# Chained top-k mask, attention, GRU and transformer block: how four stages hand over tiles

## The chip, the cores and the metric

The kernel runs on one core of a Trainium2 chip. The core has TensorE (matrix multiply), VectorE, ScalarE, GpSimd and SyncE, which issues the DMAs. The metric is the device time of one execution in microseconds (us), and lower is better. Times of a kernel are given as the median of its runs. One more execution is recorded by the hardware profiler, and all rows come from it.

## The reference, cut to what matters

Inputs: `x` is 4 x 512 x 512, float32 (B = 4 batches, T = 512 rows, D = 512 columns), with one side value per row and one condition vector per batch.

```python
x = x + top_k_mask(side * cond * softmax(x) / sqrt(512), k=5120)    # per batch: 1 where among the 5120 largest, diagonal left out
# small attention: 16 heads of 32
xn  = rms_norm(x, g_norm) * (1 + scale(cond)) + shift(cond)
q, k, v = split(xn @ W_qkv)                  # per head
q, k = rms_norm(q, g_q), rms_norm(k, g_k)
o = softmax(q @ k.T / sqrt(32)) @ v
x = x + o + o @ W_out
# GRU over the 512 rows, all batches in step, state h of 512
r = sigmoid(gi_r + (h @ W_hr + b_hr)); z = sigmoid(gi_z + (h @ W_hz + b_hz))
n = tanh(gi_n + r * (h @ W_hn + b_hn));  h = (1 - z) * n + z * h      # 512 steps, one after the other
x = x + all h
# transformer block: 16 heads of 128, MLP of 2048, all with condition-made shift, scale and gate
x1 = layernorm(x) * (1 + scale1) + shift1
x  = x + gate1 * (attention(x1 @ W_qkv + b) @ W_out + b_out)
x2 = layernorm(x) * (1 + scale2) + shift2
x  = x + gate2 * (gelu(x2 @ W_1 + b_1) @ W_2 + b_2)
```

## The kernel before

The program is a row of phases with a barrier between them: `topk_phase`, `small_attention_phase`, `split_weights`, `gate_input_phase`, `gru_phase`, `dit_condition_phase` and `dit_phase`. Each engine has its own instruction list in a phase and they meet by semaphores. A float32 operand of a product is held as a high and a low float16 part, and `products` (lines 400 to 402) does three matmuls for each product. A tile is 128 rows; a batch has TT = 4 tiles of rows and KD = 4 tiles of columns. `PE` is TensorE, `DVE` VectorE, `ACT` ScalarE, `POOL` GpSimd.

**Small attention** (from line 662). For each batch PE makes 12 projections into two PSUM banks in turn: q and k of tile 0, 1, 2, 3 (8 of them), then v of the four tiles. ACT copies each out (L903). For each tile POOL squares q and k together (L776) into the single buffer `small_tmp`, DVE sums the squares by head (L990) and adds the epsilon, ACT takes the root (L889), DVE inverts it and scales q and k (L1002, L1004, L1006). ACT then writes the high parts of q and of k, each twice (L897, four instructions), since a head's operand holds four slots of 32 columns. DVE writes the low parts, each twice (L1015, four instructions). The third v projection waits until DVE has read the first v out of its bank (L984). When all is there PE turns q and k of the first head (L818) and the heads run. POOL, after the squares of a batch, normalizes the rows of the next (L766) and then splits a quarter of the later weights (L1242, L1254, L1258) until the next batch's squares.

**GRU** (from line 1262). 512 steps. The columns of the state are two halves, a and b; the gates r, z, n of either half have a PSUM bank each. A step on PE is 4 matmuls that bring the input terms of r and z (L1334) and 96 matmuls of 4 or 8 columns with their own weight loads (L1343 low weights, L1353 high weights), in an order written out by hand: 48 before the last part of the state (`lo_b`) is needed, 48 after. DVE sums the parts of each bank (L1473, six times a step) into SBUF; for n the sum goes to `candidate`, beside the bias of h and the input term of n that ACT copied there (L1423). A scan over three slots for each value then makes `gi_n + r * sum` (L1477), ACT takes the tanh (L1431, L1438), and two more scans make the high float16 part of the new state (`hi_a`, `hi_b`, which PE waits for) and the float32 state.

**Transformer block** (from line 1616). One loop over four batches. `norm(...)` is done for all four tiles of a batch at once: statistics (L1910, L1914), root on ACT (L1853), `xn` (L1921), 16 transposes on PE (L1753), scale and shift (L1925), high part on ACT (L1856), low part on DVE (L1929). It runs twice in a batch: at its start on `X`, which SyncE loads when the previous batch's output is stored, and between the output projection of attention and the MLP. After the heads PE transposes the attended rows of tile t (L1817, 16 transposes) and projects tile t-1 (48 matmuls of 512 columns). DVE gates each projected tile (L1959), POOL adds the bias and X (L1735, L1737), and only when four tiles are there can the statistics end. Then the MLP: 16 groups of 12 matmuls of 512 columns, GELU on ACT (L1894), and a product of 48 matmuls for each tile, gated and added on DVE (L1983, L1987).

## Time and profile before

| | us |
|---|---|
| median of 3 runs | 4401.15 (4399.44 to 4403.91) |
| profiled execution | 4401.88 |
| its span, first to last instruction | 4400.2 |
| before the span's start and after its end | 1.7 |
| PE busy | 3783.8 (86%) |
| DVE busy | 2851.0 (65%) |
| ACT busy | 2073.5 (47%) |
| POOL busy | 518.8 (12%) |
| top-k | 0 to 311 |
| small attention | 311 to 1010 |
| weights and gate inputs | 1010 to 1188 |
| GRU | 1188 to 2639 |
| condition of the block | 2639 to 2704 |
| transformer block | 2704 to 4400 |

The stages are read from the first and last start of the instructions that belong to them. They follow one another, so each is a sum of its own: a stage is shorter only if the chain that ends it is. A row of a timeline is one instruction, or a run of like ones with their count; what stands in brackets is how long the engine had been idle and who ended that.

### The profile page before, as it was taken

What the parts mean: (1) busy time and instruction counts of PE and PEld (TensorE: products, weight loads), DVE (VectorE), ACT (ScalarE), POOL (GpSimd) and SP (SyncE); (2) the same over time, 40 slices, a digit from 0 to 9 for tenths busy, and PEclk for the clock granted to TensorE, in tenths of its full rate; (3) what the DMA queues carried; (4) which work ended last, traced back from release to release, by engine and by line L of the source; (5) the groups of instructions that cost most, each with busy time, mean ns of one, the idle gap of its engine ahead of it and who ended that gap; (6) DMA issues with size and microseconds to landing.
All of it is one profiled execution on the core that took longest, in us unless ns stands there. A gap on an engine that the chain in (4) does not pass through costs nothing. (4 is left out here: it accounts for less than half of the span.)

```text
span 4400.2 us, 179947 instructions
## 1 busy us (share of the span) xinstructions
PE 3783.8 (86%) x69948; PEld 2810.5 (64%) x69948; DVE 2851.0 (65%) x11559; ACT 2073.5 (47%) x7517; POOL 518.8 (12%) x425
## 2 busy tenths in 40 slices
PE   1527787776899999999999996998899889988998
PEld 0424464453599999999999992564366436634653
DVE  7888887885677777777777773573266227623752
ACT  2016585685755555555555550452154215422532
POOL 3007366360000000000000000001000100010001
PEclk9999998998855555555555558999899989998999
DMA  2002132131000000000000006200220121023102
GB/s 86 0 24 92 37 105 76 47 107 58 2 6 6 6 6 6 6 6 6 6 6 6 6 5 240 77 29 39 110 81 24 79 113 43 20 81 120 43 13 83
DMA packets 114609, 209.63 MB, mean 48 GB/s; under 512 B 44154, under 2 KB 76922, under 8 KB 112000
## 3 DMA queue, kind: packets, MB, share of 16 engines
q1 hardware_dynamic: 114436, 207.35, 13.7%
q8 instruction: 106, 1.74, 0.2%
q14 instruction: 67, 0.55, 0.0%
HBM read 165.35 MB, written 33.57 MB: 45 GB/s over the span
## 5 line engine op out<-in xcount | busy, mean ns | idle before, releaser
L514 ACT ACTIVATE dit_prob<-dit_bank,dit_head_nbias 128x512 f32<-128x512 f32 x256 | 176.0, 688 | 348.8 <-DVE dit_head_nbias L532 348.4
L1343 PE MATMUL gru_sum_na<-gru_state_parts,w_hh_lo 128*128 128x4 f16 x4096 | 262.3, 169 | 0.0
L1477 DVE TENSOR_TENSOR_SCAN gru_state_parts<-gru_keep_gate,gru_new_and_old 128x24 f16<-128x24 f32 x1024 | 212.7, 208 | 71.1
L1353 PE MATMUL gru_sum_na<-gru_state_parts,w_hh_hi 128*128 128x8 f16 x4096 | 254.9, 169 | 0.0
L1353 PE MATMUL gru_sum_ra<-gru_state_parts,w_hh_hi 128*128 128x8 f16 x4096 | 254.9, 169 | 0.0
L1353 PE MATMUL gru_sum_za<-gru_state_parts,w_hh_hi 128*128 128x8 f16 x4096 | 254.9, 169 | 0.0
L1343 PE MATMUL gru_sum_za<-gru_state_parts,w_hh_lo 128*128 128x4 f16 x4096 | 252.1, 166 | 0.0
L1343 PE MATMUL gru_sum_zb<-gru_state_parts,w_hh_lo 128*128 128x4 f16 x4096 | 252.1, 166 | 0.0
L1343 PE MATMUL gru_sum_nb<-gru_state_parts,w_hh_lo 128*128 128x4 f16 x4096 | 252.1, 166 | 0.0
L1343 PE MATMUL gru_sum_rb<-gru_state_parts,w_hh_lo 128*128 128x4 f16 x4096 | 252.1, 166 | 0.0
L1343 PE MATMUL gru_sum_ra<-gru_state_parts,w_hh_lo 128*128 128x4 f16 x4096 | 252.1, 166 | 0.0
L1477 DVE TENSOR_TENSOR_SCAN gru_n_in<-gru_reset_gate,gru_candidate 128x24 f32<-128x24 f32 x1024 | 213.0, 208 | 45.9
L1353 PE MATMUL gru_sum_nb<-gru_state_parts,w_hh_hi 128*128 128x8 f16 x4096 | 236.8, 169 | 0.0
L1473 DVE TENSOR_REDUCE gru_r_in<-gru_sum_ra 128x8 f32<-128x16 f32 x512 | 89.7, 175 | 224.0 <-PE gru_sum_ra L1353 224.0
L1731 POOL TENSOR_TENSOR dit_gated_bias<-dit_gates,dit_bias_rows 128x1024 f32<-128x1024 f32 x4 | 9.4, 2342 | 1906.9 <-DMA dit_gates<-gates 1906.9
L1441 ACT ACTIVATE gru_hist<-gru_state 128x16 f32 x512 | 118.8, 232 | 232.9 <-DVE gru_state L1477 232.9
L496 PE MATMUL small_bank<-ident,small_prob 128*128 128x128 f32 x1024 | 167.7, 288 | 68.9 <-DVE small_turned L631 43.8
L208 PE MATMUL edge_part<-ones,edge_mask 128*128 128x1 f16 x2176 | 79.7, 166 | 160.1 <-DVE edge_mask L297 152.4
L1666 PE MATMUL dit_bank<-dit_qk 128*128 128x512 f16 x768 | 207.6, 379 | 1.4 <-DVE dit_qk L1941 1.4
L400 PE MATMUL dit_bank<-dit_yh,dit_w_qk 128*128 128x512 f16 x512 | 194.1, 379 | 6.9 <-DVE dit_V L1936 6.9
L1343 PEld LDWEIGHTS gru_sum_na<-gru_state_parts,w_hh_lo 128*128 128x128 f16 x4096 | 188.1, 105 | 17.6
L625 ACT ACTIVATE small_prob<-small_bank,small_head_nmax 128x512 f32<-128x512 f32 x256 | 176.5, 690 | 42.9 <-DVE small_head_nmax L526 38.0
(315 smaller groups left out, 13410.5 us busy)
## 6 DMA issues: line engine op xcount, KB each, us to landing
dit_w_qk<-w_qk_parts SPq DMA_DIRECT2D x64, 512.0 KB, 3.6
weights<-w_parts SPq DMA_DIRECT2D x8, 4096.0 KB, 12.1
weights<-w_out_parts SPq DMA_DIRECT2D x5, 4096.0 KB, 17.5
...
```

Source lines behind the costliest of these rows:

```text
L208: mm = pe.matmul(part[g][:, j:j + 1], mask[:, g * 2 + j, c * P:(c + 1) * P], const["ones16"][:, 0:1], start=(c == 0), stop=(c == E // P - 1))
L400: pe.matmul(out, lh, rh, start=start, stop=False)
L496: mm = pe.transpose(self.PT[t % 2][:, s * P:(s + 1) * P], self.prob[:, t % 2, s * P:(s + 1) * P], self.ident)
L514: act.activation(self.prob[:, t % 2, :], self.S[t % 2], ACT.Exp, bias=bias[:, t:t + 1], scale=self.scale, accum_out=self.rsum[:, t:t + 1]) ...
L625: act.activation(self.prob[:, t % 2, :], self.S[t % 2], ACT.Exp, bias=self.nmax[:, t:t + 1], accum_out=self.rsum[:, half, j:j + 1]).then_i ...
L1343: mm = pe.matmul(bank[:, j * 2 * B:j * 2 * B + B], w_hh[1][:, k, c:c + P], parts[:, par, 0, k, :, LAST], start=opens, stop=False, skip_gro ...
L1353: mm = pe.matmul(bank[:, j * 2 * B:(j + 1) * 2 * B].rearrange("p (e b) -> p e b", e=2), w_hh[0][:, k, c:c + P], parts[:, par, :, k, :, LAS ...
L1441: act.activation(hist[:, :, :, at(i)].rearrange("p f b o -> p f (b o)"), state[:, 1 - par, :, :, LAST], ACT.Copy).then_inc(kept, 1)
L1473: return dve.tensor_reduce(out, columns.rearrange("p (f e b) -> p f b e", e=2, b=B), AX.X, ALU.add)
L1477: return dve.tensor_tensor_scan(line(out), line(factor), line(term), 0.0, ALU.mult, ALU.add)
L1666: mm = pe.matmul(s, qk[:, hs.parity, 0, qe, t * P:(t + 1) * P], qk[:, hs.parity, 1, ke, :], start=(qe + ke == 0), stop=(qe == 1))
L1731: pool.tensor_tensor(gb[:], gates[:], rows[:], ALU.mult).then_inc(gated, 1)
```

## The change

There are four parts; arithmetic and results are meant to be the same.

1. **Top-k phase.** Two small parameter loads and the making of the condition's scale and shift move here from the start of small attention. DVE prepares factors (5 small instructions after the search), ACT applies them as it reads the sums out of PSUM (8 small instructions).
2. **Small attention.** The squares move from POOL to ACT, one instruction each for q and k. The second copy of each low part is an ACT copy of the first and no longer a second DVE subtraction. POOL begins a batch's share of rows and weights only when the batch's low parts are done, so beside the heads.
3. **GRU.** The n banks hold four values for each output: the two sums that PE writes, the bias, and the input term, which ACT writes into PSUM for the next step. The scan runs over these four directly (with factors 0, 1, 1, r). DVE's two sums into `candidate` and their waits go. The order of the 96 matmuls is new: 44 stand before `lo_b` is needed, 52 after, and the second half of n is wholly at the end.
4. **Transformer block.** The second norm goes tile by tile between the output projections: the transposes of tile t-1 stand in the middle of the projection of tile t, and the first four MLP groups are done for the first 384 columns before the last tile's 128. The row tile's bias and X are added beforehand. The first norm of the next batch is done before and during the MLP product of the present one, from a second buffer `given` that SyncE fills early. The last batch is written out apart from the loop.

```diff
 topk_phase
+            for f in range(2 * KD):
+                act.activation(mod[:, f, :], emb_sum[:, f, :], ACT.Identity, scale=emb_scale[:, f:f + 1],
+                               bias=emb_shift[:, f:f + 1]).then_inc(mod_made, 1)
...
 small_attention_phase, POOL
             for b in range(B):
-                for t in range(TT):
...
-                    pool.tensor_tensor(tmp[:].rearrange("p a d -> p (a d)"), raw[:, t].rearrange("p a d -> p (a d)"),
-                                       raw[:, t].rearrange("p a d -> p (a d)"), ALU.mult).then_inc(square_ready, 1)
+                pool.wait_ge(lo4_done, (b + 1) * TT * 2)
                 if b + 1 < B:
                     norm_rows(b + 1)
                 store.pool(pool, b)
 small_attention_phase, ACT
+                def low_again(t):
+                    for j, dst in enumerate((q4, k4)):
+                        act.wait_ge(lo4_done, b * TT * 2 + t * 2 + j + 1)
+                        src, to = (2, 3) if j == 0 else (1, 3)
+                        act.activation(dst[:, t, :, to, :], dst[:, t, :, src, :], ACT.Copy).then_inc(lo4_again, 1)
...
                     act.activation(dst, qkv_bank[n % 2][:], ACT.Copy, scale=scale).then_inc(bank_free, 1)
+                    if j < QK:
+                        act.wait_ge(bank_free, b * 12 + n + 3)
+                        if j == 0:
+                            act.wait_ge(ssq_ready, b * TT + t + 1)
+                        act.activation(tmp[:, j, :], dst, ACT.Square).then_inc(square_ready, 1)
                     if QK <= n < first_v:
                         (root, high_parts)[j](t - 1)
+                    if n > QK and n < first_v and j == 0:
+                        low_again(t - 2)
                     if n == first_v:
                         root(TT - 1)
+                        low_again(TT - 2)
                     if n == first_v + 1:
                         high_parts(TT - 1)
+                low_again(TT - 1)
 gru_phase, PE (a step)
+                    low(rb, R_GATE, second, first, par)
+                    low(za, Z_GATE, first, first, par)
+                    low(ra, R_GATE, first, first, par)
+                    low(zb, Z_GATE, second, first, par)
+                    pe.wait_ge(gn_ready, i + 1)
+                    low(na, N_GATE, first, first, par, opens=True)
                     pe.wait_ge(lo_a, i + 1)
+                    high(za, Z_GATE, first, first, par)
+                    high(na, N_GATE, first, first, par)
+                    high(ra, R_GATE, first, first, par)
                     pe.wait_ge(hi_b, i + 1)
+                    low(ra, R_GATE, first, second, par)
+                    high(zb, Z_GATE, second, first, par)
+                    low(za, Z_GATE, first, second, par)
                     pe.wait_ge(lo_b, i + 1)
+                    high(ra, R_GATE, first, second, par).then_inc(ra_sum, 1)
+                    high(na, N_GATE, first, second, par)
+                    high(za, Z_GATE, first, second, par).then_inc(za_sum, 1)
+                    low(rb, R_GATE, second, second, par)
+                    low(na, N_GATE, first, second, par).then_inc(na_sum, 1)
+                    high(zb, Z_GATE, second, second, par)
+                    high(rb, R_GATE, second, first, par)
+                    high(rb, R_GATE, second, second, par).then_inc(rb_sum, 1)
+                    low(zb, Z_GATE, second, second, par).then_inc(zb_sum, 1)
+                    high(nb, N_GATE, second, second, par, opens=True)
+                    low(nb, N_GATE, second, second, par)
+                    high(nb, N_GATE, second, first, par)
+                    low(nb, N_GATE, second, first, par).then_inc(nb_sum, 1)
 gru_phase, ACT (between the keep gate and the tanh of half a)
+                    copy_gi_n(i + 1, 1 - par)
 gru_phase, DVE
+                    dve.wait_ge(r_a, i + 1)
                     dve.wait_ge(na_sum, i + 1)
-                    total(cand[:, par, A, :, 0], na_bank).then_inc(u_a, 1)
-                    dve.wait_ge(r_a, i + 2)
-                    dve.wait_ge(u_a, i + 2)
-                    dve.wait_ge(gn_ready, i + 2)
-                    chain(n_in[:, A], reset[:, A], cand[:, par, A]).then_inc(n_in_a, 1)
+                    chain(n_in[:, A], reset[:, A], n_terms[:, par, 0]).then_inc(n_in_a, 1)
...
                     chain(new_parts[:, 0, A], keep[:, A], mix[:, A]).then_inc(hi_a, 1)
+                    chain(new[:, A], keep[:, A], mix[:, A]).then_inc(state_a, 1)
                     dve.wait_ge(nb_sum, i + 1)
-                    total(cand[:, par, Z, :, 0], nb_bank).then_inc(u_b, 1)
 dit_phase, PE
+                for t in range(1, TT):
+                    if t + 1 < TT:
+                        turn_heads(t + 1)
+                    project_out(t, low_heads)
+                    turn_tile(t - 1)
+                    project_out(t, high_heads)
...
+                pe.wait_ge(tile_yl, b * TT + TT - 1)
+                for j in range(4):
...
+                    hidden(j, j, 0, early)
+                    if j == 1:
+                        turn_tile(TT - 1)
+                pe.wait_ge(tile_yl, b * TT + TT)
+                for j in range(4):
+                    hidden(j, j, early, T).then_inc(hid_sum, 1)
...
+                for t in range(TT):
+                    pe.wait_ge(mlp_gated, b * TT + t + 1)
...
+                    mm.then_inc(mlp_sum, 1)
+                    if t == 0 and more:
+                        turn_rows(b + 1)
 dit_phase, DVE
+                low_heads(0)
+                low_heads(1)
+                add_attention(0)
+                for t in range(1, TT):
+                    if t + 1 < TT:
+                        low_heads(t + 1)
+                    modulated_tile(t - 1)
+                    add_attention(t)
+                modulated_tile(TT - 1)
...
+                if more:
+                    normed_rows(b + 1)
                 for t in range(TT):
                     dve.wait_ge(mlp_sum, b * TT + t + 1)
...
+                    if t == 0 and more:
+                        modulated_rows(b + 1)
```

`add_attention(t)` gates a tile, adds X, takes its statistics, asks ACT for the root and writes `xn` of the tile; `modulated_tile(t)` applies scale and shift to four 128 x 128 squares and, after ACT's high part, writes the low part. The first projection of a batch's v now waits for the last gated tile of the batch before (`mlp_gated`).

## Rows read from the trace of the kernel before

**Rows 1.** Windows: stretch, its length, busy us of PE, PEld, DVE, ACT, POOL, clock, DMA.

```profile
330.00:383.50 53.50, 35.36 (x144) 14.40 (x144) 39.01 (x45) 17.53 (x34) 29.93 (x21) 0.87 0.10 30
...
3016.70:3034.60 17.90, 3.54 (x17) 3.17 (x16) 14.58 (x23) 4.01 (x6) 12.97 (x10) 0.69 0.58 234
...
1188.00:2639.00 1451.00, 1445.61 (x51200) 1420.94 (x51200) 1080.47 (x8210) 848.79 (x5121) 0.00 (x0) 0.50 0.03 6
```

**Rows 2.** Timeline of all engines, one GRU step.

```profile
1801.97 0.27 PE L1343 MATMUL gru_sum_na<-gru_state_parts,w_hh_lo 128*128 128x4 f16 x4
...
1803.27 0.25 PE L1353 MATMUL gru_sum_ra<-gru_state_parts,w_hh_hi 128*128 128x8 f16 x4
...
1803.56 0.17 DVE L1473 TENSOR_REDUCE gru_r_in<-gru_sum_ra 128x8 f32<-128x16 f32 x1 [0.44 <-PE gru_sum_ra L1353]
...
1803.76 0.21 ACT L1426 ACTIVATE gru_reset_gate<-gru_r_in 128x8 f32<-128x8 f32 x1 [0.17 <-DVE gru_r_in L1473]
...
1804.04 0.21 DVE L1477 TENSOR_TENSOR_SCAN gru_n_in<-gru_reset_gate,gru_candidate 128x24 f32<-128x24 f32 x1
...
1804.28 0.22 ACT L1431 ACTIVATE gru_new_and_old<-gru_n_in 128x8 f32<-128x8 f32 x1
...
1804.53 0.21 DVE L1477 TENSOR_TENSOR_SCAN gru_state_parts<-gru_keep_gate,gru_new_and_old 128x24 f16<-128x24 f32 x1
...
1804.79 0.27 PE L1343 MATMUL gru_sum_na<-gru_state_parts,w_hh_lo 128*128 128x4 f16 x4
```

**Rows 3.** Waits of PE in the block: us in total, times, longest us.

```profile
PE dit_bank L1753 <- DVE dit_big L1921: 107.5, 8, 17.6
```

**Rows 4.** Timeline, PE, from attention's output to the MLP of the first batch.

```profile
2967.39 4.52 PE L1817 MATMUL dit_bank<-ident,dit_big 128*128 128x128 f32 x32 [0.45 <-DVE dit_big L546]
...
3016.46 0.38 PE L402 MATMUL dit_bank<-weights,dit_qk 128*128 128x512 f16 x1
...
3034.61 0.61 PE L400 MATMUL dit_bank<-dit_yh,weights 128*128 128x512 f16 x1 [3.84 <-DVE dit_yl L1929]
...
3040.80 0.38 PE L400 MATMUL dit_bank<-dit_yh,weights 128*128 128x512 f16 x1
```

**Rows 5.** Timeline, PE and DVE, from the first batch of the block to the second.

```profile
3124.67 0.38 PE L402 MATMUL dit_bank<-weights,dit_V 128*128 128x512 f16 x1
...
3125.09 0.69 DVE L1983 SCALAR_TENSOR_TENSOR dit_prob<-dit_bank,dit_gates 128x512 f32<-128x512 f32 x1 [8.84 <-PE dit_bank L402]
...
3148.41 0.61 PE L400 MATMUL dit_bank<-weights,dit_yh 128*128 128x512 f16 x1 [3.71 <-DVE dit_yl L1929]
...
3153.37 0.38 PE L400 MATMUL dit_bank<-weights,dit_yh 128*128 128x512 f16 x1
```

**Rows 6.** Timeline of small attention's first batch: ACT, POOL, DVE and PE.

```profile
334.73 0.60 ACT L903 ACTIVATE small_raw<-small_bank 128x512 f32<-128x512 f32 x1 [4.51 <-PE small_bank L402]
...
343.18 2.08 POOL L776 TENSOR_TENSOR small_tmp<-small_raw 128x1024 f32<-128x1024 f32 x1 [3.24 <-ACT small_raw L903]
...
343.43 2.38 DVE L1006 TENSOR_TENSOR small_raw<-small_raw,small_rq 128x512 f32<-128x512 f32 x1
...
383.61 0.38 PE L818 MATMUL small_qbank<-ident,small_q 128*128 128x128 f16 x4 [1.69 <-DVE small_vl L984]
```

**Rows 7.** Groups by line in small attention: count, busy us, mean ns, idle before.

```profile
L903 ACT ACTIVATE small_raw<-small_bank 128x512 f32<-128x512 f32 x32 | 18.8, 588 | 57.1 <-PE small_bank L402 57.1
L897 ACT ACTIVATE small_q<-small_raw 128x512 f16<-128x512 f32 x32 | 18.4, 621 | 31.1 <-DVE small_raw L1004 31.1
L990 DVE TENSOR_REDUCE small_ssq<-small_tmp 128x32 f32<-128x1024 f32 x16 | 19.4, 1212 | 35.2 <-POOL small_tmp L776 35.2
L1002 DVE TENSOR_TENSOR small_raw<-small_raw,small_rq 128x512 f32<-128x512 f32 x16 | 11.1, 692 | 0.6
L867 ACT ACTIVATE small_tmp<-X 128x512 f32 x16 | 10.1, 630 | 41.6 <-PEq L59 39.5
```

**Rows 8.** Groups by line, DVE, 300 to 312: count, busy us, mean ns.

```profile
L377 DVE TENSOR_TENSOR_SCAN edge_rank<-edge_key,edge_before,edge_zeros 128x512 f32<-128x512 f32 x3 | 3.8, 1277 | 0.0
```

475 lines of the change are left out of this document (262 added, 213 removed).

## The prediction

> **What bounds the kernel now.** I read the windows by stage first, then the waits of PE, then the timelines around the places where PE stands still. The stages follow one another, so each is judged by its own chain.
>
> In the GRU PE is busy 1445.61 of 1451.00 us, at a granted clock of 0.50, the lower level of 1.2 GHz [rows 1]. Busy PE is not proof of a bound, so the timeline of one step decides: the step starts with the low matmuls of na at 1801.97 and the next one at 1804.79, 2.82 us later [rows 2]. In it 48 matmuls run from 1801.97 to 1803.27, 27 ns each. After 1803.27 there are 48 more and 4 that bring inputs, 52 x 27 ns = 1.40 us, but the next step starts only after 1.52. So PE waits about 0.12 us a step for the chain of the gates: PE and that chain are nearly level.
>
> In the transformer block PE stands still at two kinds of places. Its transposes of the normed rows waited 107.5 us for DVE in 8 waits [rows 3]: twice a batch, once between the output projection of attention and the MLP, and once at the start of a batch. The first is 17.9 us long with PE busy for 3.54 and DVE for 14.58 [rows 1, 4], the second runs from 3124.67 to 3148.41 [rows 5]. After either stall the matmuls run slower: 512 columns take 0.41 us each in the mean of the first 15 ((3040.80 - 3034.61)/15) and again 0.41 in the first 12 of the next batch ((3153.37 - 3148.41)/12), and 0.216 from there on.
>
> In small attention the projections of a batch are bound by neither of these: PE is busy 35.36 of 53.50 us, DVE 39.01 [rows 1]. From the first copy out of PSUM at 334.73 to the turning of the first head at 383.61 there are 48.9 us [rows 6], while PE needs 12 x 12 x 0.216 = 31.1 for the matmuls. The chain is the one of the squares, sums, scales and parts of each tile, on DVE, ACT and POOL. The heads after it are not touched.
>
> **Top-k and the condition.** DVE gets five small instructions on its path, some 0.2 us each; small attention loses about as many from its start, but there ACT's squares of rows set the start anyway. Sum: +1 us, from 0 to +2.
>
> **Small attention.** The POOL squares leave. Their price is double: the instruction itself (2.08 us), and DVE's product beside it, 2.38 us at 343.43 for a form that has a mean of 0.69 in the same stage [rows 6, 7]. The Trainium skill, SBUF — State Buffer (SBUF: two separate sides), says that GpSimd and a VectorE instruction with two SBUF inputs exclude each other for a whole instruction; with the rows either way, it only says why, and that the block's head instructions, which read PSUM, would not suffer from the POOL work that now lies fully beside them.
>
> The new turn of a tile, from DVE's sum of one tile to that of the next, is a chain across ACT and DVE, since there is one buffer of squares: sum 1.21, square of the next q 0.63, two second low copies 2 x 0.59, copy of the next k 0.59, its square 0.63, four high copies 4 x 0.62, the last low part 0.69. That is 7.4 us [rows 7]; ACT's second low copies are new, priced as the copy of the same size. The first sum starts one projection, a copy and a square after 334.73's counterpart: 2.6 + 0.59 + 0.63 = 3.8. Three turns are 22.2, with 0.6 for the first, which waits for PE. The last tile: sum 1.21, root and inversion about 0.7 (estimate), three products 2.07, low part of v 0.69, then the two v projections that had to wait, 5.2, a copy and a low part 1.28, and 0.3 to the turning: 11.4. Sum 38.0 against 48.9, so 10.9 less a batch, 4 x 10.9 = 43 us. Bounds: if nothing but the two excluded instructions is saved the gain is 20; if PE were the bound, 31.1 + 3, it is 59. I take 43. POOL now begins the weights when the low parts are done. Its quarter must end before the next batch's heads; it had over 50 us of room, and only the rows of the next batch (four instructions) are needed before, at the end of the heads. What is behind its new wait is hidden.
>
> **GRU.** The chain that ends late, read as starts in the timeline [rows 2]: ra matmuls 1803.27, sum 1803.56, sigmoid 1803.76, scan 1804.04, tanh 1804.28, scan of the high part 1804.53, PE 1804.79. In steps: 0.29 + 0.20 + 0.28 + 0.24 + 0.25 + 0.26 = 1.52.
> - The scan no longer waits for a second sum of DVE itself. It goes by the sigmoid, which lets a follower go 0.25 after its start, as the tanh does: -0.03. The last na matmuls start 16 x 27 = 0.43 after ra's; 0.29 later is 0.72, when the sigmoid is ready (0.29 + 0.20 + 0.25 = 0.74). So no new wait.
> - The scan has 32 elements for 24. A scan of 512 takes 1277 ns and one of 24 takes 0.21 us [rows 2, 8], 2.2 ns an element, so +0.02. It reads PSUM, which no scan in this trace does: from 0 to +0.10; I take +0.02, since the sum of 16 from PSUM takes only 0.17.
> - ACT copies the next input term just before the tanh: the tanh waits perhaps 0.04. The trace has no write of ACT into PSUM. The Trainium skill, ScalarE: Activation LUTs (Step-by-step: what each stage is for), calls PSUM the faster destination; no row here shows it.
>
> So the chain is 1.52 - 0.03 + 0.04 + 0.04 = 1.57 and PE's own 52 + 4 matmuls are 56 x 27 = 1.51: the wait of PE is nearly gone because eight matmuls more fit behind the ra sum. Before `lo_b` 44 matmuls are left: 1.19. Step: 1.57 + 1.19 = 2.76, or 2.74 if the copy is hidden. Late next would be `lo_b`: its chain begins with the scan of nb at 1.57 (nb's last group at 1.29, + 0.28), then tanh 0.26, high scan 0.25, state scan and subtraction 0.34, and 0.22 to PE: 2.64, needed at 2.74. It fits by 0.1. I take 2.75, and for the step before the mean of 2.82, as shown, and 1451.00/512 = 2.83: 0.078 x 512 = 40 us less. Bounds: PE's floor is 100 x 27 = 2.71, 56 us less; with the two unknown costs at their ends, 0.
>
> **Transformer block.** (a) Between projection and MLP: PE's last matmul starts at 3016.46, so PE is free at 3016.68; the MLP starts at 3034.61 [rows 4]: 17.9 us. The 16 transposes remain, now between projections: 4.52/32 x 16 = 2.3. The first 15 MLP matmuls take 6.19 us where 15 x 0.216 = 3.24 would do, and these 2.95 go with the stall. 17.9 - 2.3 + 2.95 = 18.6. What covers the moved work: DVE has a projection of 48 x 0.216 = 10.4 plus 4.5 us of transposes for a tile, and its work for one (four low parts 2.8, gating, addition, statistics, `xn` about 3.9, the tile's scale and low part 2) is about 9. `xn` of a tile is ready 3.9 us after its projection, needed at 5.2 in mid-projection. For the last tile two partial MLP groups, 2 x 12 x 0.162 = 3.9, lie before its transposes, so the wait is 0 to 0.5, and two more groups cover the rest. 384 and 128 columns cost the same as 512. Sum: 4 x 18.6 = 74.
> (b) From batch to batch: PE is free at 3124.89 and restarts at 3148.41, 23.5 us [rows 5]. What stays is the wait for the last gating (3125.09 + 0.69, so 0.9 to 1.0) and 2.3 of transposes; with 3153.37 - 3148.41 = 4.96 for 12 matmuls that cost 2.5 at 0.216, another 2.4 goes. 23.5 - 1.0 - 2.3 + 2.4 = 22.6, three times: 68. The load of X, some 6 us of the stall, is done during the heads. DVE's norm stands before the gating of the MLP's first tile, 10.4 us of PE time, and takes about 6; scale and parts take another 6, during the second tile.
> Sum 142. Bounds: if the clock drops all the same, 7 x 2.7 = 19 less; if each handover waits 1 to 2 us, 12 less; so 111. Upward 147. Last batch and first start keep their time.
>
> **The sum.** Profiled execution 4401.88 (span 4400.2 and 1.7 around it; the median is 4401.15): + 1 - 43 - 40 - 142 = 4177.9; from the median, 4177.
>
> **Rivals.**
> - Forecast: all parts come about as costed, 4177 (4145 to 4210). Chance 0.62.
> - The GRU gives nothing: PSUM scan and ACT's copy take the 0.06 to 0.10 that the order brings. For it: both costs are unseen in this trace and the chain has no room. Against: the sums of DVE read PSUM in 0.17. 4177 + 40 = 4217, with a small rest lost elsewhere up to 4250. Chance 0.22.
> - The handovers move more than they give: tile norms wait and the clock falls again, 31 us in the block; the ACT chain in small attention gives only 20, 23 more: 4231. For it: ACT has 10 instructions in a turn. Chance 0.09.
> - The clock in the GRU rises. The Trainium skill, TensorE: Matmul & The Clock Gate (Part 1: The HAM clock gate), ties the full clock to sustained activity, and by that rule PE should long be at 2.4 GHz here; the rows show 0.50 with PE busy for 99.6%, so the trace disagrees. As a mechanism of this kernel: with the 0.12 us wait gone the clock goes to 1.00, PE's side halves and the chains remain, 1.26 to the high scan of a and at least 1.2 from it to `lo_b`: a step of 2.46. Then 0.28 x 512 = 145 more: about 4030. Chance 0.02.
> - PE's floor everywhere: GRU 56, small attention 59: 4177 - 16 - 16 = 4145 or less. Chance 0.02 beyond the forecast's range.
> - Slower than before: the n scan waits for PSUM. If reading the n bank costs a step over 0.08 us the GRU loses, and the whole loses only when that cost reaches (4401 - 4177)/512 = 0.44 us. A scan of 0.65 us for 0.21 would do it; at a cost of 0.50 the time is 4177 + 256 = 4433. Nothing in the trace has such a price. Chance 0.03, a third of it within 0.2%.
> - It doesn't do what it says: the first-tile MLP wait or the weight load of `w_v` keeps the batches apart. That load starts when the last MLP group is done, 45 us ahead; 4177 + 68 = 4245. It is in the third case's chance.
>
> The forecast's own range, the second and third case and PE's floor together need 4130 to 4250; below it stands a GRU at 2.4 GHz, above it the sums of two failures and the slower case. A measurement of this kernel tells 0.2%, 9 us, from no change. Faster 0.97, same 0.01, slower 0.02.
>
> **What would show it.** GRU steps of about 2.74 us with PE starting its low matmuls within 0.05 of the last bring; the n scan at 0.23 to 0.25 us; six DVE sums become four. PE's waits on norm transposes from 107.5 us to under 20, and 0.216 spacing right at the start of the MLP and of the later batches. Projections of a small-attention batch in 42 to 44 us and L1006's counterpart at 0.69. Wrong would be: a clock other than 0.50 in the GRU, an n scan over 0.3 us, or PE waiting for ACT's second low copies long after the last v.

## The result, and the profile after

The changed kernel takes 4211.17 us (median of 4, 4207.77 to 4212.9); the kernel before, beside it, 4402.53 (4399.44 to 4406.57). The ratio is 0.9565, 95% interval 0.9552 to 0.9578. The forecast was 4177 in a range of 4130 to 4250: the direction and the size hold, and 34 us of the gain are missing. The time alone does not single out the forecast: it lies 1 us above the forecast's own 4145 to 4210 and 6 us below the rival in which the GRU gives nothing (4217). The stages do. The profiled execution took 4210.57, its span 4208.9.

The stages come one after the other, so the difference of the spans, 191.3 us, splits without a rest. Each stage is cut at rows that both traces have: ACT's first squares of X (before 311.23, after 312.22), ACT's first and last tanh of the GRU, which writes `new_and_old` (1194.42 and 2638.09; 1159.41 and 2575.18), PE's first projection of the block (2723.87; 2665.57), and the end of the span.

| stretch | before | after | difference | forecast |
|---|---|---|---|---|
| top-k, to the first squares | 311.2 | 312.2 | +1.0 | +1 |
| small attention, weights, gate inputs | 883.2 | 847.2 | -36.0 | -43 |
| GRU loop, first to last step | 1443.7 | 1415.8 | -27.9 | -40 |
| last step to the block's first projection | 85.8 | 90.4 | +4.6 | 0 |
| block, to the end | 1676.3 | 1543.3 | -133.0 | -142 |

No single term failed by much; four each gave less than their price. The windows of the changed kernel (stretch, length, busy us of PE, PEld, DVE, ACT, POOL, clock, DMA) answer [rows 1]:

```profile
330.44:375.64 45.20, 35.31 (x152) 14.85 (x153) 23.48 (x40) 26.64 (x51) 8.40 (x8) 0.95 0.01 3
1159.00:2575.00 1416.00, 1414.52 (x51134) 1403.67 (x51131) 1039.92 (x7162) 824.67 (x5118) 0.00 (x0) 0.50 0.03 6
2960.75:2969.30 8.55, 8.55 (x55) 5.18 (x54) 5.18 (x12) 2.12 (x3) 0.78 (x1) 1.00 0.93 368
3050.90:3052.00 1.10, 0.01 (x1) 0.02 (x2) 0.97 (x2) 0.00 (x0) 0.00 (x0) 1.00 0.08 15
```

The first is batch 0 of small attention, from the first projection to the first score product: VectorE is busy for half of it. The second is the GRU, still at a clock of 0.50, the level of 1.2 GHz. The third is the passage from attention's output to the MLP, where TensorE stood still for most of 17.9 us and is now busy throughout. The fourth is a batch boundary: 1.1 us of idleness where 23.5 were lost [rows 5].

One step of the GRU, timeline of all engines, answers [rows 2]:

```profile
1903.21 0.25 PE L1366 MATMUL gru_sum_ra<-gru_state_parts,w_hh_hi 128*128 128x8 f16 x4
...
1903.49 0.17 DVE L1495 TENSOR_REDUCE gru_r_in<-gru_sum_ra 128x8 f32<-128x16 f32 x1 [0.44 <-PE gru_sum_ra L1366]
...
1903.70 0.22 ACT L1446 ACTIVATE gru_reset_gate<-gru_r_in 128x8 f32<-128x8 f32 x1 [0.51 <-DVE gru_r_in L1495]
...
1903.99 0.22 DVE L1499 TENSOR_TENSOR_SCAN gru_n_in<-gru_reset_gate,gru_sum_n 128x32 f32<-128x32 f32 x1
...
1904.13 0.17 ACT L1435 ACTIVATE gru_sum_n<-gi_n 128x16 f32 x1
...
1904.24 0.22 ACT L1452 ACTIVATE gru_new_and_old<-gru_n_in 128x8 f32<-128x8 f32 x1
...
1904.49 0.21 DVE L1499 TENSOR_TENSOR_SCAN gru_state_parts<-gru_keep_gate,gru_new_and_old 128x24 f16<-128x24 f32 x1
...
1904.76 0.27 PE L1356 MATMUL gru_sum_rb<-gru_state_parts,w_hh_lo 128*128 128x4 f16 x4
...
1905.95 0.25 PE L1366 MATMUL gru_sum_ra<-gru_state_parts,w_hh_hi 128*128 128x8 f16 x4
```

From ra to the low matmuls are 1.55 us (forecast 1.57), from there to the next ra 1.19 (forecast 1.19): 2.74. The step inside the loop is what was forecast. But the mean of the loop is 1415.8/511 = 2.77. TensorE's first bring (the matmul that brings the input terms) of each step shows where the rest is:

```profile
1899.16 0.19 PE L1339 MATMUL gru_sum_za<-gru_gi_now,gru_scaled_ident 128*128 128x16 f16 x1
...
1901.85 0.17 PE L1339 MATMUL gru_sum_za<-gru_gi_now,gru_scaled_ident 128*128 128x16 f16 x1
...
1904.60 0.17 PE L1339 MATMUL gru_sum_za<-gru_gi_now,gru_scaled_ident 128*128 128x16 f16 x1
...
1907.33 0.17 PE L1339 MATMUL gru_sum_za<-gru_gi_now,gru_scaled_ident 128*128 128x16 f16 x1
...
1910.23 0.19 PE L1339 MATMUL gru_sum_za<-gru_gi_now,gru_scaled_ident 128*128 128x16 f16 x1
```

Steps of 2.69, 2.75, 2.73 and 2.90 us: the fourth goes over the end of TensorE's loop, which holds four steps. The bring after it starts early again, so the price of the edge is read from the chain, at ACT's tanh of half a:

```profile
1909.73 0.22 ACT L1452 ACTIVATE gru_new_and_old<-gru_n_in 128x8 f32<-128x8 f32 x1
...
1912.57 0.22 ACT L1452 ACTIVATE gru_new_and_old<-gru_n_in 128x8 f32<-128x8 f32 x1
```

These two lie 2.84 us apart, across an edge. Over the whole loop the starts of this tanh are 2.746 us apart inside TensorE's loop and 2.838 across its end: an edge costs 0.09 us. In the kernel before every step has 2.823, edge or not.

In the block, PE's waits (total, times, longest) answer [rows 3]:

```profile
PE dit_bank L1789 <- DVE dit_big L2022: 21.8, 1, 21.8
...
PE dit_bank L414 <- DMA dit_w_qk<-w_qk_parts: 4.3, 3, 2.2
```

The eight waits of 107.5 us are down to the one at the block's start (21.8, where the prediction's sign was under 20), and a new one has come: for the weights of head 2. The timeline of SyncE's queue shows what is ahead of them, and TensorE's rows the wait, in batches 0 and 2:

```profile
2708.66 0.33 SPq L1731 DMA_DIRECT2D weights<-w_parts  x1
2709.31 0.40 SPq L1735 DMA_DIRECT2D dit_given_x<-x_gru  x1
2715.91 0.35 SPq L1721 DMA_DIRECT2D dit_w_qk<-w_qk_parts  x1
```

```profile
2725.85 0.39 PE L414 MATMUL dit_bank<-dit_yh,dit_w_qk 128*128 128x512 f16 x1 [0.98 <-DMA dit_w_qk<-w_qk_parts]
...
3497.14 0.39 PE L414 MATMUL dit_bank<-dit_yh,dit_w_qk 128*128 128x512 f16 x1 [2.25 <-DMA dit_w_qk<-w_qk_parts]
```

The 1 MB of the next batch's rows (`given`) is new between the MLP's weights and head 2's. The last batch has no such load and no such wait.

At the block's start the first norm is slower. DVE and POOL after:

```profile
2652.59 1.26 POOL L1768 TENSOR_TENSOR dit_gated_bias_rest<-dit_gated_bias 128x512 f32<-128x512 f32 x1
2653.81 5.65 POOL L1772 TENSOR_TENSOR dit_X<-dit_given_x,dit_gated_bias 128x512 f32<-128x512 f32 x4
```

```profile
2653.03 5.31 DVE L2022 TENSOR_SCALAR dit_big<-dit_given_x,dit_mv,dit_rstd 128x512 f32<-128x512 f32 x4
```

Before, the same four `xn` took 1.91 us there, where GpSimd was idle, and 5.12 in the middle of the batch, where it worked:

```profile
2714.64 1.91 DVE L1921 TENSOR_SCALAR dit_big<-dit_X,dit_mv,dit_rstd 128x512 f32<-128x512 f32 x4
...
3022.19 5.12 DVE L1921 TENSOR_SCALAR dit_big<-dit_big,dit_mv,dit_rstd 128x512 f32<-128x512 f32 x4
```

So the price stood in the trace of before; the forecast did not look for what the moved GpSimd work would lie beside.

### The profile page after: what moved, and what is told of

Its sections match the earlier page's. It is cut to its first block and busy times, and to the rows that moved or that the text cites. A ratio compares the mean times of both kernels' runs of the same rounds, so it can differ in the third digit from the quotient of the medians.

```text
span 4208.9 us, 177781 instructions
## 1 busy us (share of the span) xinstructions
PE 3731.0 (89%) x70140; PEld 2793.1 (66%) x70140; DVE 2778.2 (66%) x10585; ACT 2086.6 (50%) x7601; POOL 461.4 (11%) x397
## 5 line engine op out<-in xcount | busy, mean ns | idle before, releaser
L1366 PE MATMUL gru_sum_n<-gru_state_parts,w_hh_hi 128*128 128x8 f16 x8192 | 500.2, 175 | 0.0
L1356 PE MATMUL gru_sum_n<-gru_state_parts,w_hh_lo 128*128 128x4 f16 x8192 | 489.4, 168 | 0.0
L1366 PEld LDWEIGHTS gru_sum_n<-gru_state_parts,w_hh_hi 128*128 128x128 f16 x8192 | 376.7, 104 | 0.0
L1356 PEld LDWEIGHTS gru_sum_n<-gru_state_parts,w_hh_lo 128*128 128x128 f16 x8192 | 376.7, 104 | 0.0
L1499 DVE TENSOR_TENSOR_SCAN gru_n_in<-gru_reset_gate,gru_sum_n 128x32 f32<-128x32 f32 x1024 | 225.5, 220 | 54.6
L1356 PE MATMUL gru_sum_rb<-gru_state_parts,w_hh_lo 128*128 128x4 f16 x4096 | 261.3, 169 | 0.0
L1366 PE MATMUL gru_sum_zb<-gru_state_parts,w_hh_hi 128*128 128x8 f16 x4096 | 254.5, 169 | 0.0
L1446 ACT ACTIVATE gru_reset_gate<-gru_r_in 128x8 f32<-128x8 f32 x512 | 111.4, 218 | 272.5 <-DVE gru_r_in L1495 272.5
L414 PE MATMUL dit_bank<-weights,dit_V 128*128 128x512 f16 x512 | 196.5, 384 | 10.3 <-DVE dit_V L2115 10.3
```

The costliest lines, as they stand in the source:

```text
L414: pe.matmul(out, lh, rh, start=start, stop=False)
L1356: mm = pe.matmul(columns[:, j, 0], w_hh[1][:, k, c:c + P], parts[:, par, 0, k, :, LAST], start=opens, stop=False, skip_group_check=True)
L1366: mm = pe.matmul(columns[:, j], w_hh[0][:, k, c:c + P], parts[:, par, :, k, :, LAST], start=opens, stop=False, skip_group_check=True)
L1446: act.activation(reset[:, A, :, GATED], r_in[:, A], ACT.Sigmoid, scale=1.0 / GS).then_inc(r_a, 1)
L1499: return dve.tensor_tensor_scan(line(out), line(factor), line(term), 0.0, ALU.mult, ALU.add)
```

## Experiments

Every kernel was read in its own stage, cut as in the table above. The GRU repeats best: the eight kernels with the changed GRU loop have it at 1415.8 to 1416.3 us. Where nothing was changed in them, the start of the block takes 89.5 to 90.4 us, the block 1540.9 to 1543.3, small attention with weights and gate inputs 845.7 to 850.7, and its four batches together 177.0 to 179.3 us to their first scores, of which the changed kernel has the lowest. So a difference of 2 us in that sum is no effect.

**1. The loop edge: `edge8`.** TensorE's loop of the GRU holds 8 steps.

```diff
 gru_phase
-        NOW = 2
+        NOW = 4
```

> The changed kernel, with TensorE's loop in the GRU holding 8 steps instead of 4 (64 loop edges for 128). Theory (loop edge): in the trace of the changed kernel three of four steps take 2.69 to 2.75 us and the one across the loop edge 2.91, so an edge costs about 0.13 us that the old chain used to hide; 64 edges fewer give 64 x 0.13 = 8 us: GRU loop 1415 to about 1407 us, whole 4211 to about 4203. Rival (chain): the 0.024 us a step over 2.745 is spread over all steps as a longer gate chain, and the time stays at 4211. Rival (code): the longer loop body brings its instructions slower and the GRU gets slower than 1415.

Measured: 4201.46 us (4200.14 to 4202.63), ratio to before 0.954 (0.9524 to 0.9555). The GRU loop is 1407.5, 8.3 less, as the first theory said. The price by edge was not as it said: the step across an edge now takes 2.796 us and the others 2.746, so an edge of the longer loop costs 0.05 us where the shorter one's cost 0.09. 127 edges of 0.092 are 11.7 us and 63 of 0.050 are 3.2: 8.5 less, for the 8.3 measured. 0.13 is only what went for each edge that is gone. Why the edge of the longer loop is cheaper stays open. The edit also halves the number of loads of input terms that TensorE waits for, but in the changed kernel the step with such a wait and no edge takes 2.745 us, so that wait costs nothing. Another 2.4 us are in the block, where nothing was changed (see experiment 2 for what varies there).

**2. The new load: `given_late`.** The rows of the next batch are loaded after the heads' weights.

```diff
 dit_phase, SyncE
-                if more:
-                    sp.wait_ge(a_begun, (b + 1) * TT)
-                    sp.wait_ge(xn_ready, (b + 1) * TT)
-                    sp.dma_start(given[:], ...)
                 with sp.Fori(0, (H - 2) // 2) as pair:
...
+                if more:
+                    sp.wait_ge(a_begun, (b + 1) * TT)
+                    sp.wait_ge(xn_ready, (b + 1) * TT)
+                    sp.dma_start(given[:], ...)
```

> The changed kernel with the load of the next batch's rows (1 MB) issued after the heads' weight loads instead of between the 4 MB load of the MLP weights and the load of head 2's weights. Theory (queue): the rows stand ahead of head 2's weights and delay them; TensorE waits 1.0, 1.1 and 2.25 us for them in three batches, and the heads take 1.2, 1.3 and 4.1 us longer than before: all of 6.6 us goes, whole about 4204, no wait of TensorE on those weights. Rival (the 4 MB load alone does it): the wait stays at about 1 us each and the time at 4209 to 4211.

Measured: 4201.59 us (4200.64 to 4202.4), ratio 0.9539 (0.9523 to 0.9555). TensorE waits for no head's weights. From the first head's projection to the second MLP product the batches take 294.3, 294.3, 294.3 and 294.2 us, in the changed kernel 295.4, 295.5, 298.4 and 294.2: 6.5 us, the number of the theory. Of these 4.3 are the waits themselves; after the longest one, 2.25 us in batch 2, the matmuls came 0.43 us apart from 3498.04 on, for 0.216, which is most of the rest. The block gains 11.3 in all (1543.3 to 1532.0). The other 4.8 lie behind another wait: the MLP's second product begins after 2.6 us of idleness in both kernels, and in the changed one seven or eight matmuls near its start come 0.43 us apart in batches 0, 1 and 3, in this one they all come at 0.216. Windows of PE (length, busy, clock, DMA) over those matmuls, first the changed kernel, then this one:

```profile
3005.80:3012.00 6.20, 6.20 (x21) 0.72 0.98 423
...
3778.75:3789.10 10.35, 10.35 (x48) 1.00 0.83 356
```

```profile
3007.74:3014.00 6.26, 6.26 (x29) 1.00 0.97 419
```

The same idleness lets the clock fall in one batch and not in the next. What decides it isn't settled; it makes the block vary by a few us between kernels that don't touch it.

**3. GpSimd beside the first norm: `pool_waits`.**

```diff
 dit_phase, GpSimd
                 pool.wait_ge(gated, b * 2 + 1)
+                pool.wait_ge(yl_ready, (b + 1) * KD)
                 pool.tensor_tensor(gb_rest[:], gb[:, 1, :], gb[:, 0, :], ALU.subtract).then_inc(gated, 1)
```

> The changed kernel, in the block: GpSimd's additions of bias and rows (one of the two biases, then four tiles) wait until VectorE has the low parts of the normed rows. Theory (shared port): in the changed kernel the four xn of the first batch take 5.31 us beside these additions and took 1.91 before; they go back to 1.9, TensorE's first projection of the block comes 3.4 us earlier after the last GRU step (90.4 to about 87 us), whole about 4207. Rival (memory): the xn are slow because the new loads write into SBUF at that time; nothing changes, 90 us.

Measured: 4208.32 us (one run). The stretch before the block's first projection is 86.7 for 90.4 (89.5 to 90.4 in the kernels that leave it alone), and the four `xn` are back:

```profile
2654.26 1.91 DVE L2023 TENSOR_SCALAR dit_big<-dit_given_x,dit_mv,dit_rstd 128x512 f32<-128x512 f32 x4
```

The loads are the same in both, so it is GpSimd's work. The Trainium skill, SBUF — State Buffer (Who interferes with whom), says that `tensor_scalar` can run in a mode that takes the port pair shared with GpSimd, so that the later of the two waits for the whole instruction. The trace agrees: 5.31 and 5.12 us beside GpSimd, 1.91 and 1.91 without. The forecast had drawn on this page only for instructions with two inputs.

**4. The order of the GRU's matmuls undone, the scan kept: `scan_old_order`.** The 96 matmuls, and DVE's two sums of rb and zb, stand as before: 48 matmuls ahead of `lo_b`, na right after ra and za, nb in two places.

```diff
 gru_phase, PE
-                    low(rb, R_GATE, second, first, par)
-                    low(za, Z_GATE, first, first, par)
-                    low(ra, R_GATE, first, first, par)
-                    low(zb, Z_GATE, second, first, par)
                     pe.wait_ge(gn_ready, i + 1)
                     low(na, N_GATE, first, first, par, opens=True)
+                    low(rb, R_GATE, second, first, par)
+                    low(zb, Z_GATE, second, first, par)
+                    low(nb, N_GATE, second, first, par, opens=True)
+                    low(ra, R_GATE, first, first, par)
+                    low(za, Z_GATE, first, first, par)
...
```

> The changed kernel with the order of the GRU's 96 matmuls (and of the two sums of rb and zb) as in the kernel before; the scan over PSUM stays. Theory (order pays): the gate chain stays at 1.55 us and 48 matmuls instead of 44 stand before lo_b, 1.30 for 1.19 us: step 2.85, GRU loop about 1456 us (after: 1415, before: 1443), whole about 4252: the scan in PSUM without the order is worth nothing or less. Rival (scan pays): what helped is that VectorE makes two sums fewer; the order matters little, GRU loop 1415 to 1420, whole 4211 to 4216.

Measured: 4235.99 us (one run), GRU loop 1439.1, a step of 2.81. It is neither theory's number, but the order carries most: 23.3 of the 27.9 us go with it, and the scan alone is worth 4.6. Inside TensorE's loop the order is worth more, 2.813 for 2.746 or 34 us; 11 of them are paid at the loop edges, which the old order hides (2.818 across an edge). The expected 1456 took the chain of the new order, 1.55; in this order it is shorter:

```profile
1802.64 0.25 PE L1366 MATMUL gru_sum_ra<-gru_state_parts,w_hh_hi 128*128 128x8 f16 x4
...
1803.38 0.22 DVE L1499 TENSOR_TENSOR_SCAN gru_n_in<-gru_reset_gate,gru_sum_n 128x32 f32<-128x32 f32 x1 [0.18 <-ACT gru_reset_gate L1446]
...
1804.15 0.27 PE L1356 MATMUL gru_sum_n<-gru_state_parts,w_hh_lo 128*128 128x4 f16 x4
```

The scan comes 0.74 after ra, right behind the sigmoid, and the low matmuls after 1.51. In the new order it came after 0.78: there the last matmuls of na begin at 1903.63, later than here (1802.85, 0.21 after ra). So the new order pays about 0.04 for na's place and wins 4 matmuls, 0.11, ahead of `lo_b`.

**5. The new order without the scan: `order_alone`.** The kernel before with the new order; DVE still sums n into SBUF.

```diff
 gru_phase, PE and DVE of the kernel before
+                    low(rb_bank, R_GATE, second, first, par)
+                    low(za_bank, Z_GATE, first, first, par)
...
+                    high(ra_bank, R_GATE, first, second, par).then_inc(ra_sum, 1)
+                    high(na_bank, N_GATE, first, second, par)
...
+                    low(nb_bank, N_GATE, second, first, par).then_inc(nb_sum, 1)
...
+                    chain(new[:, A], keep[:, A], mix[:, A]).then_inc(state_a, 1)
                     dve.wait_ge(nb_sum, i + 1)
                     total(cand[:, par, Z, :, 0], nb_bank).then_inc(u_b, 1)
```

> The kernel before with the new order of the 96 matmuls in the GRU and VectorE's work in the matching order; n is still summed into SBUF by VectorE. Theory (the scan makes the order possible): nb now ends the step, and its sum (about 0.2 us) lies before the scan of n, so the low part of b is ready 2.64 + 0.2 = 2.84 us after the ra matmuls begin: step 2.83 to 2.86, GRU loop 1443 to 1460 us, no gain over the kernel before (whole 4400 to 4420). Rival (order alone pays): step 2.75 or less, GRU loop about 1410 to 1415, whole about 4373.

Measured: 4514.31 us (one run), GRU loop 1554.9, 111 more than before. The theory's direction holds, its size doesn't. The step is 3.04, not 2.84:

```profile
1803.90 0.25 PE L1353 MATMUL gru_sum_ra<-gru_state_parts,w_hh_hi 128*128 128x8 f16 x4
...
1804.61 0.18 DVE L1473 TENSOR_REDUCE gru_candidate<-gru_sum_na 128x8 f32<-128x16 f32 x1
...
1804.87 0.21 DVE L1477 TENSOR_TENSOR_SCAN gru_n_in<-gru_reset_gate,gru_candidate 128x24 f32<-128x24 f32 x1
...
1805.63 0.27 PE L1343 MATMUL gru_sum_rb<-gru_state_parts,w_hh_lo 128*128 128x4 f16 x4
```

The sum of na, which the old order hid behind the sigmoid, now starts at the sigmoid's end: the scan comes 0.97 after ra and the low matmuls 1.73. The second half is late as well, 1.31 for 1.19; nb's sum, now at the end of the order, lies ahead of it. So the two edits of the GRU don't add: +111 and -4.6 alone, -27.9 together. The scan is what makes the order possible.

**6. The squares back on GpSimd: `pool_squares`.** ScalarE's squares and GpSimd's wait go, GpSimd's loop over tiles is as before. So GpSimd's rows and weights, too, lie beside VectorE's work again.

```diff
 small_attention_phase
             for b in range(B):
-                pool.wait_ge(lo4_done, (b + 1) * TT * 2)
+                for t in range(TT):
+                    pool.wait_ge(bank_free, b * 12 + place_of[t, 1] + 1 + 2)
+                    pool.wait_ge(ssq_ready, b * TT + t + 1)
+                    pool.tensor_tensor(tmp[:].rearrange("p a d -> p (a d)"), raw[:, t].rearrange("p a d -> p (a d)"),
+                                       raw[:, t].rearrange("p a d -> p (a d)"), ALU.mult).then_inc(square_ready, 1)
...
-                        act.activation(tmp[:, j, :], dst, ACT.Square).then_inc(square_ready, 1)
...
```

> The changed kernel with the squares of small attention back on GpSimd (one instruction a tile into the same buffer, and GpSimd's rows and weights right after them, as before); ScalarE keeps the second low copies. From the first projection of a batch to its first score product the changed kernel takes 45.2, 43.8, 44.0 and 44.1 us, the kernel before 54.9, 53.6, 53.6 and 51.2. Theory (squares): nearly all of the difference is the square and the product that stands still beside it, so 8 to 9 us a batch come back, 52 to 54 us, whole 4240 to 4246. Rival (VectorE's load): the squares are half of it, 4 to 5 us a batch, whole about 4229.

Measured: 4227.4 us (one run). The batches take 51.4, 48.5, 49.5 and 48.2 us to their first score: 6.2, 4.7, 5.5 and 4.1 more, 20.5 together. This is the rival's number. By groups of DVE (count, busy us, mean ns, idle before), the product beside the square, first in the changed kernel, then here:

```profile
L1014 DVE TENSOR_TENSOR small_raw<-small_raw,small_rq 128x512 f32<-128x512 f32 x16 | 10.9, 683 | 0.0
```

```profile
L1014 DVE TENSOR_TENSOR small_raw<-small_raw,small_rq 128x512 f32<-128x512 f32 x16 | 33.0, 2060 | 0.0
```

The mechanism is as told, 0.68 us becomes 2.06, but it is not the whole: squares and exclusion, with GpSimd's rows and weights beside VectorE (its low parts take 0.87 and 0.93 us for 0.69), are a little over half of the small part's gain.

**7. The second low copies back on VectorE: `copies_on_dve`.**

```diff
 small_attention_phase, DVE
-                        slot = 2 if j == 0 else 1
-                        dve.tensor_tensor(dst[:, t, :, slot, :], src, dst[:, t, :, 0, :], ALU.subtract)\
-                           .then_inc(lo4_done, 1)
+                        for e in range(2):
+                            slot = 2 + e if j == 0 else 1 + 2 * e
+                            ins = dve.tensor_tensor(dst[:, t, :, slot, :], src, dst[:, t, :, 0, :], ALU.subtract)
+                        ins.then_inc(lo4_done, 1)
...
 small_attention_phase, ACT
-                    if n > QK and n < first_v and j == 0:
-                        low_again(t - 2)
...
```

> The changed kernel with the second low copies of q and k in small attention back on VectorE as second subtractions; squares stay on ScalarE. Theory (a chain that alternates): a tile's turn gives 2 x 0.61 us of ScalarE for 2 x 0.69 of VectorE, nearly level; projections to first score 44 to 46 us a batch, whole 4211 to 4216. Rival (VectorE is the bound): its 2 x 0.69 us a tile come on top, 5.5 us a batch, 49 to 50 us, whole about 4232.

Measured: 4217.91 us (one run); batches of 47.9, 46.4, 45.8 and 44.6 us, 7.6 together. It lies between, near the first theory. The first score again comes 1.37 us after the turning, for 1.80. With experiment 6 that makes 28 of the 36.3 us of the four batches. The rest, 8 us, was not taken apart; experiment 6 has GpSimd's rows and weights back in their place already, so it belongs to the two edits together (in the kernel before VectorE's doubled low parts lie beside GpSimd and take 0.91 and 0.99 us each), if it is not scatter.

**8. The weights beside the products: `weights_early`.** GpSimd's wait for the low parts goes.

```diff
 small_attention_phase, GpSimd
             for b in range(B):
-                pool.wait_ge(lo4_done, (b + 1) * TT * 2)
                 if b + 1 < B:
                     norm_rows(b + 1)
                 store.pool(pool, b)
```

> The changed kernel without GpSimd's wait for the low parts: a batch's share of rows and weights starts with the projections and lies beside VectorE's products instead of beside the heads. Theory (exclusion): each of VectorE's 20 instructions with two SBUF inputs of a batch waits about 1 us for a GpSimd instruction (0.6 to 1.5 us each); its products take 1.2 to 2 us for 0.69, a batch's projections 55 to 65 us for 44, whole 4255 to 4290. Rival (no contention of that size): the products stay at 0.7 us and the time at 4208 to 4213.

Measured: 4233.18 us (one run), small attention and gate inputs 870.9 for 847.2. A batch takes 50.4, 48.7, 47.6 and 45.2 us to its first score, and the first three periods from batch to batch are 7.9 to 8.4 longer. It is neither theory's number: contention is there, and the whole loses 22 us where at least 44 were expected, so the waits aren't one whole instruction each. Means over four batches, in the last of which GpSimd has little to do, by groups of DVE:

```profile
L1013 DVE TENSOR_TENSOR small_raw<-small_raw,small_rq 128x512 f32<-128x512 f32 x16 | 15.6, 976 | 0.0
...
L1000 DVE TENSOR_SCALAR small_ssq<-small_ssq 128x32 f32<-128x32 f32 x16 | 11.4, 710 | 0.6
```

The smallest instruction suffers most: the scalar step on 32 elements takes 710 ns, and 181 in the changed kernel, where GpSimd waits.

**9. The next batch's norm after the MLP: `serial_rows`.** The calls for norm, transposes and parts of batch b + 1 stand behind the last tile of the MLP on TensorE and VectorE; ScalarE's come in the same order as before.

```diff
 dit_phase, PE
-                    if t == 0 and more:
-                        turn_rows(b + 1)
+                if more:
+                    turn_rows(b + 1)
 dit_phase, DVE
-                if more:
-                    normed_rows(b + 1)
                 for t in range(TT):
...
-                    if t == 0 and more:
-                        modulated_rows(b + 1)
+                if more:
+                    normed_rows(b + 1)
+                    modulated_rows(b + 1)
```

> The changed kernel with the first norm of the next batch (VectorE's norm, the 16 transposes, scale and parts) after the MLP's last tile instead of beside the MLP product; its rows are still loaded early. Theory (the norm was the stall): a boundary gets back the gating and sum 1.4, the norm 5.9, transposes to first projection 7.4 us, less 3.0 that stand there now, and 0 to 2.4 for the lower clock: 12 to 15 us each, three times 36 to 45; where GpSimd's additions fall beside the xn, 3.4 more each. Whole 4247 to 4266. Rival (the load was the stall): since the rows lie in SBUF early, under 5 us a boundary, whole under 4226.

Measured: 4262.45 us (one run), block 1594.5, 51.2 more. A boundary costs 17.1: 14.9 to the first projection and 2.2 of slower matmuls in it (the first one; 51.2 is three times this). The norm was the stall, not the load. GpSimd's additions fell beside the low parts instead of `xn`, 5.76 us for 2.49, the same price at another place; without these 3.3 us a boundary is within the theory's 12 to 15.

**10. Undivided MLP groups: `whole_groups`.**

```diff
 dit_phase, PE
-                pe.wait_ge(tile_yl, b * TT + TT - 1)
+                turn_tile(TT - 1)
+                pe.wait_ge(tile_yl, b * TT + TT)
                 for j in range(4):
...
-                    hidden(j, j, 0, early)
-                    if j == 1:
-                        turn_tile(TT - 1)
-                pe.wait_ge(tile_yl, b * TT + TT)
-                for j in range(4):
-                    hidden(j, j, early, T).then_inc(hid_sum, 1)
+                    hidden(j, j, 0, T).then_inc(hid_sum, 1)
```

> The changed kernel with the first four MLP groups undivided: TensorE transposes the last tile right after its projection and begins the groups with all 512 columns when that tile's low part is ready. Theory (cover): from the last projection's end at 2960.97 to the end of the last low part at 2968.35 are 7.4 us, which 48 matmuls of 384 columns cover now; without them the stall is 6.7 us a batch and up to 2.9 more if the clock falls: 27 to 38 us, whole 4238 to 4249. Rival (tile norms alone suffice): under 2 us a batch, whole under 4219.

Measured: 4242.06 us (one run), block 1576.6, 33.3 more. The two waits of the first batch are those of the sum:

```profile
2965.07 0.63 PE L1864 MATMUL dit_bank<-ident,dit_big 128*128 128x128 f32 x4 [3.86 <-DVE dit_big L2083]
...
2968.62 0.61 PE L414 MATMUL dit_bank<-dit_yh,weights 128*128 128x512 f16 x1 [2.92 <-DVE dit_yl L2094]
```

From the transposes of the first head rows to the second MLP product, the cut by which the middle gained 73 us (see below), the batches take 104.6, 104.4, 104.4 and 105.4 us for 95.4: 37 us hang on the division of the first four groups, at the upper end of the theory's 27 to 38. The block grew by less because other places ran faster: the slow matmuls of experiment 2 came in batch 3 alone, and the heads lost 4.8 us to their weights for 6.5. The other 36 us are left to the norm by tiles by subtraction; no run has it alone.

**11. Three edits at once: `all_three`.** Those of experiments 1, 2 and 3 together.

```diff
-        NOW = 2
+        NOW = 4
...
+                pool.wait_ge(yl_ready, (b + 1) * KD)
...
                 with sp.Fori(0, (H - 2) // 2) as pair:
...
+                if more:
...
+                    sp.dma_start(given[:], ...)
```

> The changed kernel with three edits at once: TensorE's GRU loop of 8 steps, the next batch's rows loaded after the heads' weights, and GpSimd's additions after the low parts. They lie in different stages, so they add: 8.3 (measured in the GRU alone) + 6.5 (three waits on head 2's weights) + 3.5 (xn beside GpSimd) = 18 us, and 0 to 5 from matmuls at the lower clock after short stalls: 4188 to 4193. Rival (they overlap): more than 4196.

Measured: 4190.22 us (4188.57 to 4195.27), ratio 0.9519 (0.9503 to 0.9535). GRU loop 1406.1, start of the block 86.7, block 1534.8: they add. It is faster than both kernels of the comparison, 21 us under the changed one.

**12. A still longer loop: `all_three_16`.**

```diff
-        NOW = 4
+        NOW = 8
```

> As the kernel with three edits, with TensorE's GRU loop of 16 steps. Theory (loop edge): 32 edges fewer than with 8 steps, 0.13 us each, 4 us less: GRU loop 1403, whole 4184 to 4189. Rival (code): bringing the longer loop body costs as much as the edges, so the GRU loop stays at 1407 or grows.

Measured: 4459.12 us (4446.26 to 4460.47), ratio 1.0119 (1.0102 to 1.0136): slower than the kernel before. The GRU loop is 1678.2. The step across an edge takes 8.41 us in the mean, which makes some 176 of the 272 us that the GRU lost; the rest is lost inside the loop. TensorE's 188 waits of over 0.3 us have no other engine behind them ("issue"), and there is none of that length in the GRU with a loop of 4 or 8 steps. The queue that brings instructions (packets, MB, share) has five times the bytes, first the kernel with 8 steps, then with 16:

```profile
q8 instruction: 114, 1.87, 0.2%
```

```profile
q8 instruction: 557, 9.13, 0.8%
```

```profile
1841.38 0.19 PE L1339 MATMUL gru_sum_za<-gru_gi_now,gru_scaled_ident 128*128 128x16 f16 x1 [3.10 <-issue]
...
1844.82 0.19 PE L1366 MATMUL gru_sum_zb<-gru_state_parts,w_hh_hi 128*128 128x8 f16 x1 [2.13 <-issue]
```

The rival was right, far beyond its own words. A step has 100 matmuls and 100 weight loads in the trace (51200 of each in 512 steps, [rows 1]), so 8 steps are 1600 of these and 16 are 3200. The Trainium skill, Runtime: NRT & Kernel Launch (Instruction fetch mechanics), gives TensorE room for 2048 instructions and says that a taken branch whose target isn't in the part held waits for a DMA. The trace agrees with that: 114 packets with the loop of 8, and 557 with 16, 14 more for each of the 32 turns. Where between 1600 and 3200 the limit lies, no run here shows.

## Why the prediction was right, and where it fell short

**Top-k, +1.** Right: +1.0.

**Small attention, -43; measured -36.0.** The step that was mis-sized is "4 x 10.9": the price of batch 0 was taken four times. From first projection to first score the batches took 54.9, 53.6, 53.6 and 51.2 before, and 45.2, 43.8, 44.0 and 44.1 after: 9.7, 9.8, 9.7 and 7.2 less. Within batch 0 the sum was close: 38.0 forecast from the first copy to the turning of head 1, and 373.84 - 334.89 = 38.95 measured. Timelines of ACT, DVE and PE in that batch:

```profile
334.89 0.60 ACT L912 ACTIVATE small_raw<-small_bank 128x512 f32<-128x512 f32 x1 [4.35 <-PE small_bank L416]
...
369.38 0.60 ACT L912 ACTIVATE small_vh<-small_bank 128x512 f16<-128x512 f32 x1 [3.21 <-PE small_bank L416]
```

```profile
338.77 1.22 DVE L998 TENSOR_REDUCE small_ssq<-small_tmp 128x32 f32<-128x1024 f32 x1 [7.71 <-ACT small_tmp L917]
...
360.43 1.21 DVE L998 TENSOR_REDUCE small_ssq<-small_tmp 128x32 f32<-128x1024 f32 x1
```

```profile
373.84 0.38 PE L821 MATMUL small_qbank<-ident,small_q 128*128 128x128 f16 x4 [1.91 <-ACT small_k L907]
```

The first sum came after 3.9 us (forecast 3.8), three turns took 21.7 (22.2 and 0.6), the last tile 13.4 instead of 11.4. The two last projections of v were taken at 2.6 us each, but the first of them runs after 5.4 us of idleness: its copy starts 4.07 us after it, at 369.38 (it began at 365.31), and the next one 2.59 later. Before had the same stretch at the same length (8.58 us from this projection to the turning, 8.53 after), so it could have been read there. Batch 3 gave least because it was the shortest before, 51.2 us. The last row names the other part: TensorE's turn ends its wait with ScalarE's second low copy of the last k (372.99 and 0.62), some 0.3 us after the last low part of v (372.60 and 0.69). The first score then comes 1.80 us after the turning, for 1.37 before: 0.4 us more a batch.

**GRU, -40; measured -27.9.** The step itself was right: 1.57 + 1.19 against 1.55 + 1.19, the scan at 0.22 us, ACT's copy hidden, and `lo_b` in time. Inside TensorE's loop a step went from 2.823 to 2.746, which is 39 us in 511 steps. (The 40 of the sum came from 2.83, a mean with the loop's start in it; from 2.823 to its 2.75 are 37.) What failed is the loop edge, a term the sum didn't have. The old chain had 0.12 us of slack on TensorE, and the edge lay in it: in the kernel before a step across it takes the same 2.823 as any other, and in experiment 4, where the slack is back, only 0.005 more. With the slack gone a step across the edge is 0.092 longer, and 127 of them are 11.7 us, the whole of what is missing. Experiment 1 bears it out: half the edges, 8.3 us less. The reason given for the gain, more matmuls behind ra, holds (experiment 4), but what it needs was told as a small saving: without the scan the same order loses 111 us (experiment 5).

**Start of the block, 0; measured +4.6.** "Last batch and first start keep their time" was wrong. 3.4 us are the `xn` beside GpSimd (experiment 3: 2.8 to 3.7 back); the last microsecond is in the loads of the parameters, DVE's first wait 8.26 us for 7.33, and was not tested.

**Block, -142; measured -133.0.** The middle, cut from the transposes of the first head rows to the second MLP product, gave 19.2, 18.0, 18.0 and 18.0 (before 114.6, 113.5, 113.5, 113.5; after 95.4 in all four): 73.3 for 74. The boundary, from that product to the first head's projection, gave 22.6, 21.2 and 23.2: 67.0 for 68. So both stalls were priced within 2%. What was missing is the load that came with the change: it was called "done during the heads", and the queue it was put into was not followed to who comes next, head 2's weights: 1.2, 1.2 and 4.1 us, 6.5 in all (experiment 2). The end of the block has 0.8 more. In that 0.8, and in the 21.2 of the second boundary, are the slow matmuls behind the 2.6 us of idleness ahead of the second MLP product: the changed kernel has them in batches 0, 1 and 3, the kernel before in batch 0 alone. Since what decides them isn't known, a few us of the block's agreement are chance either way.

**The rivals.** The GRU that gives nothing, the weaker handovers, the slower case and the kernel that doesn't do what it says are all excluded by their stages: the GRU gave 27.9 us, the block 133.0, small attention 36.0. The clock of the GRU stayed at 0.50 with TensorE busy for 1414.52 of 1416.00 us. By the Trainium skill, TensorE: Matmul & The Clock Gate (Part 1: The HAM clock gate), an engine that busy should be at 2.4 GHz; both traces disagree. PE's floor in the GRU, 56 us less, wasn't reached either.

The four misses add up: 7 + 12 + 4.6 + 9 = 33 us, all of one sign. 12 (the edge), 4.6 and most of the 9 are waits that the change brought or laid bare, and a sum of removed waits has no line for those; the 7 of small attention are stretches that could have been read before, in batch 0 and in batch 3.
